# Layer 0's attention: where the four query blocks of half 1 and the fetch of batch 4's queries stand in the order of work

## What is computed

```python
def _L0_xattn_ref(query, key, value, Wq, bq, Wk, bk, Wv, bv, Wo, bo):
    Q = query @ Wq + bq
    K = key @ Wk + bk
    V = value @ Wv + bv
    ...
    scores = jnp.einsum('bhgqd,bhkd->bhgqk', Q, K) * scale
    w = jax.nn.softmax(scores, axis=-1)
    y = jnp.einsum('bhgqk,bhkd->bhgqd', w, V)
    y = y.transpose(0, 3, 1, 2, 4).reshape(B, S, EMBED)
    return y @ Wo + bo
...
x = x + _L0_xattn_ref(_layernorm(x, axis=-1), ctx_4096, ctx_4096, L0_xattn_Wq, ...)
```

## Time and profile before

| | |
|---|---|
| Median of 3 runs | 1216.76 us (1213.69 to 1220.43) |
| The profiled execution: time, span of its instructions | 1218.03 us, 1216.7 us |
| Mean granted TensorE clock over the span | 0.992 of full speed |
| Layer 0's attention | the first 180 us or so of the span |
| TensorE busy | 1181.7 us, 97% of the span |
| VectorE, ScalarE, GpSimd busy | 66%, 55%, 35% |

### The profile page before, as it was taken

One profiled execution on the slowest core, in us unless ns is written; L12 is line 12 of the kernel. 1 busy time (PEld: TensorE's weight loads), 2 busy tenths in 40 slices (PEclk: granted clock), 3 DMA queues, 4 the chain that ended last, 5 costly groups with the idle time before them and its releaser, 6 DMA issues.

```text
span 1216.7 us, 16554 instructions
## 1 busy us (share of the span) xinstructions
PE 1181.7 (97%) x5936; PEld 913.3 (75%) x5936; DVE 803.2 (66%) x1509; ACT 669.5 (55%) x1562; POOL 423.2 (35%) x517
## 2 busy tenths in 40 slices
PE   8899998999999999999999999999999999999999
PEld 5555555667776676788888888878888888888767
DVE  3456778677776784856666666774456666666877
ACT  2245653477777785355555555653455565556631
POOL 2503442577777783012322322320023223322300
PEclk9889999999999999999999999999999999999999
DMA  8667242685679666521111121121211121211201
GB/s 285 173 145 167 76 166 89 245 260 102 124 189 299 150 146 105 179 70 61 53 61 44 61 70 61 52 70 44 78 44 51 63 61 61 69 44 44 69 1 70
DMA packets 72849, 127.93 MB, mean 105 GB/s; under 512 B 11640, under 2 KB 30968, under 8 KB 70072
## 3 DMA queue, kind: packets, MB, share of 16 engines
q1 hardware_dynamic: 53024, 73.90, 20.0%
q0 software_dynamic: 17296, 48.26, 15.9%
q10 hardware_dynamic: 2448, 4.72, 1.1%
HBM read 150.37 MB, written 26.48 MB: 145 GB/s over the span
## 4 chain that ended last, share of the span: by engine, by line
PE 74%; POOL 7%; DVE 6%; issue 6%; DMA 4%; ACT 3%; SPq 0%; ACTq 0%; POOLq 0%; DVEq 0%
PE bank L473 48%; PE bank L2031 7%; PE bank L1223 5%; PE bank L2007 4%; POOL moe L1606 4%; PE bank L685 2%; POOL xs L1595 2%; PE bank L699 2%; PE bank L651 1%; PE bank L666 1%; POOL wf_raw L1585 1%; DMA wf_raw<-in_wffn,weight_row 1%; PE bank L2356 1%; PE bank L449 1%; PE bank L1283 1%
## 5 line engine op out<-in xcount | busy, mean ns | idle before, releaser
L1998 POOL TENSOR_SCALAR p<-p,mx 128x256 f32<-128x256 f32 x256 | 163.6, 657 | 500.4 <-DVE mx L1992 500.4
L1190 DVE TENSOR_TENSOR wf_lo<-wf_raw,wf_hi 128x512 fp32r<-128x512 f32 x188 | 121.5, 688 | 34.4 <-ACT wf_hi L1184 32.2
L1984 ACT ACTIVATE p<-bank,mx 128x256 f32<-128x256 f32 x256 | 118.1, 486 | 10.9 <-DVE mx L1974 10.8
L473 PE MATMUL bank<-xnA_hi,w1q_hi 128*128 128x512 f32 x288 | 117.7, 409 | 0.7 <-DVE w1q_lo L1773 0.7
L1184 ACT ACTIVATE wf_hi<-wf_raw 128x512 fp32r<-128x512 f32 x192 | 110.2, 626 | 10.1 <-DMA wf_raw<-in_wffn,weight_row 10.1
L473 PE MATMUL bank<-xnA_hi,w1q_lo 128*128 128x512 f32 x288 | 114.1, 396 | 0.0
L473 PE MATMUL bank<-xnA_lo,w1q_hi 128*128 128x512 f32 x288 | 113.5, 394 | 0.0
L2014 ACT ACTIVATE p1T_hi<-bank 128x512 fp32r<-128x512 f32 x128 | 75.0, 596 | 65.2 <-PE bank L2007 65.2
L1938 ACT ACTIVATE q1T_hi<-bank 128x512 fp32r<-128x512 f32 x64 | 38.3, 598 | 130.2 <-PE bank L473 130.2
L473 PE MATMUL bank<-w1o_hi,a1T_hi 128*128 128x512 f32 x256 | 105.2, 411 | 0.2 <-DVE a1T_lo L2042 0.2
L473 PE MATMUL bank<-wf_raw,zT 128*128 128x512 f32 x220 | 102.9, 593 | 2.2 <-DVE x L1266 1.7
(11 more groups left out here) (342 smaller groups left out, 2956.8 us busy)
## 6 DMA issues: line engine op xcount, KB each, us to landing
w_raw<-in_wq SPq DMA_DIRECT2D x64, 256.0 KB, 2.6
w_raw<-in_wo SPq DMA_DIRECT2D x64, 256.0 KB, 2.7
moe<-xn SPq DMA_DIRECT2D x2, 2304.0 KB, 11.7
returned<-moe SPq DMA_DIRECT2D x8, 512.0 KB, 6.4
q0st<-q_rows SPq DMA_DIRECT2D x14, 256.0 KB, 4.7
ctx<-in_ctxT SPq DMA_DIRECT2D x2, 1024.0 KB, 8.6
x<-in_x SPq DMA_DIRECT2D x8, 256.0 KB, 8.0
q_rows<-q0T_hi ACTq DMA_DIRECT2D x8, 256.0 KB
```

The costliest lines, as they stand in the source:

```text
L473: ins = nc.tensor.matmul(ps, a, b, start=(n == 0), stop=(n == len(pairs) - 1))
L1190: nc.vector.tensor_tensor(wf[m % 2][1][:, a, c, :], raw[m % STREAMS][:, a, c, :], wf[m % 2][0][:, a, c, :].bitcast(F32), ALU.subtract).the ...
L1984: ins = nc.scalar.activation(pr1[s % 2][:, h, :], banks.of(("s1", s, n))[:, hh * 2 * P:(hh + 1) * 2 * P], ACT.Exp, bias=m[:, UH + h:UH + h ...
L1998: ins = nc.gpsimd.tensor_scalar(pr1[s % 2][:, h, :], pr1[s % 2][:, h, :], m[:, 3 * UH + h:3 * UH + h + 1], 1.0, ALU.mult, ALU.mult)
```

## The change

Block 1 of half 1 is computed ahead of the main loop, behind block 0, in bank 5 instead of 7. Blocks 2 and 3 take the units 10 and 12, where blocks 1 and 2 stood; nothing is left at unit 19. ScalarE issues the stores of blocks 0 and 1 at units 2 and 4, those of 2 and 3 at 11 and 13. VectorE takes block 0's remainder before the first maxima and block 1's behind the maxima of unit 2. On SP the queries of batch 4 are fetched before the transfer of batch 2's maxima. No instruction is added or taken away.

```diff
-        QUERY_AT = {KV0 + 2: 1, KV0 + 4: 2, LEAD_S + 5: 3}
-        QUERY_OUT_AT = {3: 0, KV0 + 3: 1, KV0 + 5: 2, LEAD_S + 6: 3}
+        QUERY_AT = {KV0 + 2: 2, KV0 + 4: 3}
+        QUERY_OUT_AT = {2: 0, 4: 1, KV0 + 3: 2, KV0 + 5: 3}
...
             keys_in(3)
+            queries_in(4)
             maxima(2)
-            queries_in(4)
             keys_in(4)
...
             keys(1, 5)
             query(1, 0, 7)
+            query(1, 1, 5)
...
             keys(1)
             query(1, 0)
+            query(1, 1)
...
             keys(1)
+            query(1, 0)
             for i in range(-LEAD_S, UNITS0 - KV0 + ADD_LAG + 1):
                 if i + LEAD_S < UNITS0:
                     softmax_max(i + LEAD_S)
                 j = i + LEAD_S
                 if j == 2:
-                    query(1, 0)
+                    query(1, 1)
```

## The result

The changed kernel takes 1219.28 us (median of 12 runs, 1215.07 to 1224.83), beside 1216.82 (1213.69 to 1220.43) for the kernel before: ratio 1.0025, 95% interval 1.0013 to 1.0037. That is 0.25% slower, within the half per cent that the prediction called no change, but outside its range (1206.5 to 1216.5) and 8 us from its 1211.3. The profiled execution took 1218.32 us, the one of before 1218.03; so the trace shows a loss of 0.3 us, the medians one of 2.5.

What follows compares the result with a forecast made beforehand. TensorE, busy for 97% of the span, bounds the kernel, so time is won only where it idles or runs at its lower clock. +1.4 - 3.1 - 2.2 - 1.7 + 0.4 - 1.5 = -6.7 us, 1218.03 to 1211.3 us, range 1206.5 to 1216.5.

Steps and rivals of the forecast that it cites:

- Term 1: Ahead of half 1's first scores: a second query block makes them start at 45.72 instead of 44.28 us, +1.4 us.
- Term 2: Units 19 to 20: without the query block, batch 1's turned scores come sooner, less 0.5 us waiting for maxima, -3.1 us.
- Term 3: Unit 32: fetching batch 4's queries earlier removes the wait for its keys, -2.2 us, and the lower clock behind, -1.7.
- Term 4: Unit 24's turned scores, behind unit 36: batch 3's maxima may wait behind the 1.5 MB weights, +0.4 us, bounds 0 and 2.7.
- Term 5: Opening, 44 to 55 us: with the idle 1.87 us filled, less lower clock, -1.5 us, bounds 0 and -3.4.
- The sum: Whole kernel: all gains and costs together give -6.7 us from the profiled 1218.03 us, so 1211.3 us.
- The clock staying up: Opening at 2.4 GHz throughout: 1209.4 us, or about 1207 if the stretch around 70 gains too; chance 0.27.
- Unit 32 still waiting: Batch 4's keys stay late for other reasons than the queries ahead, 2.18 and 1.7 us stay: 1214.8 us; chance 0.20.
- A new wait for batch 1's maxima: Unit 20: maxima land near 78 us behind stores, losing 3.55 us plus 3.4 of clock: 1219.3 us; chance 0.08.

Runs made afterwards that it cites:

- profiles side by side: Four profiles of kernels with the query blocks as before against eight with the changed blocks, up to unit 24: the changed blocks give back 0.2 us.
- moved kernels: Kernels with the changed query blocks, in eight profiles, against four with the blocks as before: lower clock around 70 us takes 2.5 us instead of 1.3.
- blocks alone: Changed kernel with batch 4's queries fetched behind batch 2's maxima again: 1217.42 us, ratio 1.0003; with the shared expert's weights also in three pieces, 1217.55 us, 0.9998.
- split kernel: Changed kernel with the shared expert's 1.5 MB in three 512 KB transfers behind the maxima of batches 3, 4 and 6: 1214.27 us (0.9979), again 1213.84 (0.9975).
- pieces alone: Kernel before the change, with only the shared expert's weights cut into three transfers behind the maxima of batches 3, 4 and 6: 1216.08 us, ratio 0.9990.

## Why the prediction was wrong

**Term 1, the second block: +1.4, right.** The first scores start at 45.23, against 44.28: +1.0, without idle time (the row of the blocks, 7.11 us, runs into that of the scores). From 38.69 to 45.23 are 3.27 us a block, where I had 3.49.

**Term 2, the block at unit 19: -3.1, right in this profile, too large on the average.** The lead grows from nearly nothing at unit 19 to 3.6 us at unit 24. The maxima of batch 1 took 4.13 us and TensorE waited 0.76, where I had taken 0.5. The bounds, 0 and 3.5 us, were well placed for the other kernels: in their profiles this wait is anything from none to 5.68 us. Over the profiles side by side the stretch from unit 19 to unit 24 got 2.1 us shorter.

**Term 3, batch 4's queries: -2.2 and -1.7, right in this profile.** Unit 32 starts without idle time and 2.4 us more ahead than unit 24, and the clock behind it is 1.00 instead of 0.52; 7.4 us of lead in front of batch 3's turned scores. Here row and rule had been set against each other: the page "DMA: Bandwidth & Descriptors" of the Trainium skill, section "Specifications", has pieces of 512 bytes at the full line rate, by which the queries ahead would have held nobody up. The keys that no longer stand behind them come in time; the row decided rightly. Only the 177 GB/s that I set against the page were of a stretch (93 to 96 us) in which the first of the weights were already moving too.

**Term 4, the collision: +0.4 was the step that failed.** It measured 8.3 us. The mechanism and the place were among the predicted ones, and so were most of its times. The prediction told them in the time of before, where unit 32 starts at 93.36; in the trace it starts at 89.57, so 3.8 us have to be added to what the trace shows. I had the maxima issued near 96 (92.07 + 3.8 = 95.9) and wanted at 99.0 (95.67 + 3.8 = 99.5). At the latest the weights, and the maxima with them, were to land at 100.7 to 101.7; they landed at 100.8 + 3.8 = 104.6. Three things were wrong. First, "with less traffic ahead the weights should take less than the 8.5 us": they took 11.0, and 11.7 in the second profile. I had looked only at the traffic ahead of them, and the keys and queries behind them had come closer, from 8.8 us behind the weights' issue to 5.7. No run tests whether that made the weights slower, and the keys alone don't: with the weights moved, on the changed kernel, they follow by 1.7 us and the weights take 7.8. And SP issued the weights 0.6 us sooner (89.81 + 3.8 = 93.6), not 1 to 2. So even the bound of 2.7 us was too small, by 2.6. Second, I took a value near the lower bound, for maxima issued some 3 us behind a load of 1.5 MB (2.3 in the trace), though the trace had no like row: there the distance was 5.4 us. Third, I priced the wait and not the clock behind it, though the earlier trace rows showed 1.7 us of it lost behind a gap of 2.18: it was 3.0 us here.

**Term 5, the clock in the opening: -1.5, right.** One stretch of about 3.4 us at the lower clock instead of 6.8, so 1.7 us less lost; on the average of the profiles side by side it is 2.1 less.

**What the terms left out is the second step that failed.** The sum says of the stretch around 70 that its 3.4 us "stay as they are", and has no term for unit 8. In the first profile of the change the stretch loses 1.7 and unit 8 does not wait, so nothing shows. But the 3.4 of the profile before were no property of the kernel: two of the other three profiles with the blocks as before have a full clock there (1.00), and the moved kernels lose 1.3 us more than those four on the average. With the waits at unit 8 and with batch 1's maxima, terms 1, 2 and 5 come to 0.2 us instead of 3.2. The medians of the blocks alone (1.0003 and 0.9998) say the same.

**The sum.** Without term 4 it was -7.1, and the profile has 7.4 us of lead at batch 3's turned scores. That this fits so well is in part luck, since the lead counts from a slow opening before. -7.4 + 8.3 = +0.9 at unit 40 and +0.3 in the span. The rest of the miss is that the sum was made against a profiled execution 1.2 us above its median, and the change's profile is 1 us below its own: a single execution of this kernel is good to some 3 us. With term 4 gone, in the split kernel, the change is 2.8 to 3.7 us under before's median, and not 7.1.

**The rivals.** The clock staying up: it did from 44 to 49 and at 93, not around 52 or 70. Unit 32 still waiting: not seen with the early fetch, and seen (1.68 and 1.71 us) in the two versions without it. A new wait for batch 1's maxima: small in the changed kernel, but 2.7 to 5.7 us in four of the others (3.40 with the weights on ScalarE's queue), a late landing as described; behind which transfers is open. Its time, 1219.3, is the measured one, but not for its reason: the wait that took everything was of the same kind, two batches later and behind another transfer.

**What stays open.** Why the same 1.5 MB took 7.8 us in some profiles and 11.7 in others; what holds up batch 1's maxima in some kernels (the stores of half 1's keys are the suspect, not moved by themselves); and what makes the clock fall around 50 and 70 in one execution and not in the next.

## What to carry to other kernels

When a gap is closed, everything behind it is issued closer together, so list the large transfers next to come and price the small ones that stand behind them at the large one's landing, not at their own few us, and add the clock's loss behind a gap of several us. A large load that is needed late is better cut in pieces and spread between the small ones that are needed soon: moving it whole only moves the jam to the next transfer (ratio 1.0015), three pieces made the same change a gain (0.9979 and 0.9975, from 1.0025; the pieces alone 0.9990). A stretch of lower clock or a short wait in one profile is not yet there to be won: look for it in a second profile of the same kernel before it goes into a sum. Judge a gain of 0.3% by medians over a dozen runs; the waits of a few us for transfers differ between two profiles of the same kernel.

## What was not expected of the hardware

A transfer of 32 KB took 2.78 us by itself, 8.79 us when issued 2.3 us behind 1.5 MB on the same queue, and still 6.08 us on another queue than these 1.5 MB, 2.9 us behind them. In both cases it landed within half a us of the large one: a second queue did not keep the small transfer clear of it. The 1.5 MB took 7.8 to 11.7 us in different kernels, longest in the two profiles of the change. With a query block's stores 5 us ahead of it, one load of 128 KB of queries took 9.25 us, and in the same kernel 32 KB, issued 2.4 us behind 512 KB of stores, took 8.84. Behind a gap of 5.33 us the granted clock was 0.50 for 6 us, at full use of TensorE. The page "TensorE: Matmul & The Clock Gate" of the Trainium skill, section "Part 1: The HAM clock gate", has idleness put the clock down; this row agrees. The clock also fell around 50 and 70, where the idle times were under 1.2 us; around 70 it was 0.51 in one profile with the blocks as before, 0.76 in another and 1.00 in two, with the same order of work up to there.
